# Moving the third batch's last twenty scatters from the tail into the attention slots of a two-layer transformer kernel, and the last batch's norm ahead of them

## What is computed

```
x = _layernorm(x + _L1_attn_ref(x, ...), axis=-1)

logits = flat.astype(jnp.float32) @ router_w.T + router_bias
scores = jax.nn.softmax(logits, axis=-1)
topk_scores, topk_idx = jax.lax.top_k(scores, TOPK)      # TOPK = 4 of E = 32
```

## Time and profile before

| | us |
|---|---|
| median of 3 runs | 1424.19 (1421.38 to 1424.64) |
| the profiled execution | 1412.93 |
| its span, from first to last instruction | 1410.9 |
| TensorE busy in the span | 1062.7 |
| VectorE busy | 785.1 |
| ScalarE busy | 516.9 |
| GpSimd busy | 507.8 |
| mean granted clock of TensorE | 0.872 |

### The profile page before, as it was taken

How to read it: one execution, slowest core, us unless ns; L and a number is a source line. 1 busy time by engine, 2 the same in 40 slices (tenths; PEclk the granted TensorE clock), 3 DMA queues, 4 the chain that set the end, 5 groups by cost and what they waited for, 6 DMA issues and landing times. The chain is left out here.

```text
span 1410.9 us, 20679 instructions
## 1 busy us (share of the span) xinstructions
PE 1062.7 (75%) x6895; PEld 625.1 (44%) x6896; DVE 785.1 (56%) x2075; ACT 516.9 (37%) x814; POOL 507.8 (36%) x542
## 2 busy tenths in 40 slices
PE   5762159815899999899999989884675976667676
PEld 4661137602344444444454434422443865556443
DVE  4757820145767877778777887841431433232326
ACT  1330014312265566565666556453211311111113
POOL 3110055066035103600154114342453366665633
PEclk9975569955599999999999999997698999998998
DMA  4226015213212121311232122015231422322135
GB/s 114 81 60 116 1 35 145 71 37 106 70 27 85 46 48 34 93 37 48 66 95 67 42 72 59 21 62 232 73 95 46 108 80 80 83 73 63 36 106 193
DMA packets 90022, 106.09 MB, mean 75 GB/s; under 512 B 16883, under 2 KB 69884, under 8 KB 87286
## 3 DMA queue, kind: packets, MB, share of 16 engines
q1 hardware_dynamic: 76502, 78.49, 19.3%
q0 software_dynamic: 13072, 25.90, 6.6%
q10 hardware_dynamic: 360, 0.59, 0.1%
HBM read 63.29 MB, written 37.95 MB: 72 GB/s over the span
## 5 line engine op out<-in xcount | busy, mean ns | idle before, releaser
L2005 DVE TENSOR_REDUCE maxima<-psum 128x1 f32<-128x512 f32 (+4 forms) x624 | 390.3, 644 | 116.7 <-PE psum L1826 62.7
L1944 ACT ACTIVATE probs<-psum 128x1024 f32<-128x1024 f32 (+3 forms) x384 | 300.2, 809 | 280.9 <-PE psum L1841 218.5
L1821 PE MATMUL psum<-ka,qa 75*128 75x512 bf16 (+3 forms) x768 | 242.5, 348 | 33.4 <-DVE maxima L2005 21.2
L1837 PE MATMUL psum<-qa,ka 78*128 78x512 bf16 (+3 forms) x768 | 206.7, 332 | 4.3 <-ACT probs L1944 2.1
L116 POOL DMA_INDIRECT expert_out<-g_y,g_place x160 | 155.2, 970 | 124.0 <-DMA expert_out<-g_y,g_place 56.2
L1854 PE MATMUL psum<-probs,v_wide 128*32 128x512 f32 (+3 forms) x1536 | 167.9, 510 | 0.0
L1821 PEld LDWEIGHTS psum<-ka,qa 75*128 75x128 bf16 x768 | 68.6, 99 | 178.2 <-DVE maxima L2005 137.3
L1358 POOL DMA_INDIRECT got<-expert_out,to_row x64 | 64.9, 1015 | 162.7 <-ACT probs L1944 103.5
L2480 DVE TENSOR_TENSOR g_y<-psum,g_gate 128x512 f32<-128x512 f32 x40 | 27.7, 691 | 156.2 <-DMA expert_out<-g_y,g_place 146.5
L1837 PEld LDWEIGHTS psum<-qa,ka 78*128 78x128 bf16 x768 | 74.4, 100 | 76.2 <-ACT probs L1944 28.2
L1841 PE MATMUL psum<-mask_k,ident_b 128*128 128x128 bf16 x512 | 104.4, 224 | 0.0
(11 more groups left out here) (325 smaller groups left out, 1646.1 us busy)
## 6 DMA issues: line engine op xcount, KB each, us to landing
g_rows<-sorted SPq DMA_DIRECT2D x160, 65.0 KB, 1.9
qa<-q_steps SPq DMA_DIRECT2D x45, 192.0 KB
ka<-k_steps SPq DMA_DIRECT2D x15, 576.0 KB
f_got<-expert_out SPq DMA_DIRECT2D x16, 512.0 KB, 11.1
w<-in_W SPq DMA_DIRECT2D x16, 256.0 KB
w_gu<-in_gu SPq DMA_DIRECT2D x1, 4096.0 KB, 18.1
q_steps<-q_parts SPq DMA_DIRECT2D x12, 256.0 KB
k_steps<-k_parts SPq DMA_DIRECT2D x12, 256.0 KB
```

The source lines that it names most:

```text
L1821: mm = pe.matmul(bank[:, h * width:(h + 1) * width], qa[b][0:ROWS_MAX, h0 + h, qt * P:(qt + 1) * P], ka[b][0:ROWS_MAX, h0 + h, seg * HALF: ...
L1837: mm = pe.matmul(out, ka[s.buf][0:ROWS_ALL, h, j * P:(j + 1) * P], qa[s.buf][0:ROWS_ALL, h, q0:(c + 1) * HALF], start=True, stop=True, ski ...
L1944: act.activation(probs[k % PRING][:, 2 * pair:2 * pair + 2, 0:w], PS[:, 2 * pair:2 * pair + 2, 0:w], ACT.Exp).then_inc(exps, 1)
L2005: dve.tensor_reduce(maxima[:, seg, h0:h0 + heads, qt], bank[:, 0:heads * width].rearrange("p (h k) -> p h k", h=heads), AX.X, ALU.max).the ...
```

## The change

The tuple `Finish` gets a field `beside`, the number of scatters in one slot. It is 1 for batches 0 and 1. Batch 2 gets 2, and its `paced` goes from 12 to all 32, so slots 32 to 47 of batch 3 hold two each. In the tail, `moves` then holds the 32 scatters of batch 3 alone, and `emit_norm` comes first in GpSimd's list.

```diff
-                 softmax=(20, 20), exp=21, choose=(22, 27), count=27, place=(29, 30), pick=(31, 42), scatter=32, paced=12)
+                 softmax=(20, 20), exp=21, choose=(22, 27), count=27, place=(29, 30), pick=(31, 42), scatter=32, paced=4 * TB, beside=2)
...
-                    k, t = divmod(r - f.scatter, TB)
-                    if 0 <= r - f.scatter < f.paced:
-                        if t == 0:
-                            emit_places1(pool, S, b, k)
-                        pool.wait_ge(exps, 2 * g)
-                        emit_scatter1(pool, S, b, k, t)
+                    for m in range(f.beside):
+                        k, t = divmod((r - f.scatter) * f.beside + m, TB)
+                        if 0 <= k * TB + t < f.paced:
+                            if t == 0:
+                                emit_places1(pool, S, b, k)
+                            pool.wait_ge(exps, 2 * g)
+                            emit_scatter1(pool, S, b, k, t)
...
-                for n, (b, k, t) in enumerate(moves):
-                    if n == TB:
-                        emit_norm(pool, S, 1, LAST)
+                emit_norm(pool, S, 1, LAST)
+                for b, k, t in moves:
```

More of the change, by code:

```diff
@@ L1109 @@
 BATCH_SLOTS = QUARTERS * SLOTS
-Finish = namedtuple("Finish", "turn_att proj moments scale each turn_new logits softmax exp choose count place pick scatter paced")
+Finish = namedtuple("Finish", "turn_att proj moments scale each turn_new logits softmax exp choose count place pick scatter paced beside")
 LATER = Finish(turn_att=(12, 13), proj=(15, 16), moments=(18, 24), scale=26, each=2, turn_new=(28, 30), logits=32,
-               softmax=(34, 35), exp=36, choose=(38, 45), count=45, place=(47, 49), pick=(50, 60), scatter=52, paced=4 * TB)
+               softmax=(34, 35), exp=36, choose=(38, 45), count=45, place=(47, 49), pick=(50, 60), scatter=52, paced=4 * TB, beside=1)
 AT_ONCE = Finish(turn_att=(4, 5), proj=(7, 8), moments=(10, 12), scale=14, each=4, turn_new=(15, 16), logits=18,
-                 softmax=(20, 20), exp=21, choose=(22, 27), count=27, place=(29, 30), pick=(31, 42), scatter=32, paced=12)
+                 softmax=(20, 20), exp=21, choose=(22, 27), count=27, place=(29, 30), pick=(31, 42), scatter=32, paced=4 * TB, beside=2)
 FINISH = {0: LATER, 1: LATER, 2: AT_ONCE}
```

## The result

The changed kernel is slower. In the first measurement the ratio of its time to the kernel before is 1.0106 (95% interval 1.0063 to 1.0150), medians 1442.26 against 1422.79 us. In microseconds the two ratios are +15.1 and +5.6, with +7.7 forecast in between. The medians are taken over all executions and the ratios over the fast ones alone; of the profiled executions that of `drain_in_between` was a slow one, and `all_landed` was executed only once. Single executions of either kernel scatter over 20 to 30 us, so the timed runs alone do not settle a term of a few microseconds. The profiles do, if they are read in pieces.

A forecast was written before the change was run, and what follows sets the result against it. Taken as bounding: GpSimd, whose DRAIN blocks end on and whose late norm stalls the tail 15.0 us. 22.0 (seam) + 0.7 (clock) - 15.0 (norm) = +7.7, 1424.19 to 1431.9 us; 8-in-10 range 1427 to 1439.

The forecast's parts named there:

- The copy: Before k = 1 in slot 36: GpSimd newly waits 5.0 us for batch 2's x_alt copy, held by batch 1's odd-k scatters.
- Slots 36 to 47: End of attention: 24 scatters with 21 gaps of 1.28 us and 2 of 2.10, the last starting at 981.27.
- the fifth rival: Slots 36 to 47: the scatter burst runs slower than 1.28 us each, up to +24.3, 1448.5 us; 8 in 100.
- The DRAIN: Attention's end: GpSimd's DRAIN ends 6.8 us after its last scatter starts (6.3 to 8.2), at 988.1.
- The seam: Between attention and tail: the tail opens 22.0 us later (21.5 to 23.4), waiting for GpSimd's DRAIN.
- The start of the tail: TensorE's two turnings before the variance both take 1.09 us after its long pause: +0.7 us (0 to 1).
- The third rival: Tail's turnings and router: TensorE's clock comes back sooner, saving 2.7 us, so +5.0, 1429.2 us; 7 in 100.
- The norm: In the tail: it waits only for the variance, at 1000.2, giving back 15.0 us; scatters behind it cost nothing.
- The rest: Shared block's loads, batch 3's 32 scatters and its copy: zero together, with 1 us either way.
- The first rival: At the seam other engines don't wait for GpSimd; norm starts at 982.3, time 1413.9 us; 4 in 100.
- The second: At the seam GpSimd's DRAIN takes only 0.31 us; sum +2.2, 1426.4 us; 5 in 100.
- The fourth: Before k = 1 the copy is not waited for: -5.0, so +2.7 and 1426.9 us; 3 in 100.

The follow-up runs named there:

- drain_in_between: Changed kernel with one more GpSimd DRAIN ahead of slot 26 of batch 3; ratio to the kernel before 1.0023 (0.9977 to 1.0069).
- all_landed: Changed kernel, GpSimd waiting for all scatters of batches 0 to 2 to land before attention ends; slot 32 to tail's end 168.9 us, single execution, no ratio.
- no_drain_at_seam: Changed kernel without GpSimd's DRAIN at attention's end, event exchange kept; ratio to the kernel before 0.9972 (0.9936 to 1.0008).
- norm_first_20_left: Kernel before with only the norm moved first in GpSimd's tail list, all 20 leftover scatters behind it; ratio to the kernel before 0.9973 (0.9930 to 1.0015).

## Why the prediction was right, and where not

Its direction and its mechanism hold: the moved scatters stretch attention by more than the earlier norm gives back. Step by step, in times from the first scatter of slot 32 or from the seam:

- *Slots 32 to 35.* Batch 1's last scatter 14.08 us after the first: it was 958.60 - 944.48 = 14.12.
- *The copy.* A wait of 5.0 us: 5.12, and removing its cause took 5.2 off the seam.
- *Slots 36 to 47.* The last scatter 52.25 us after the first: 52.39. The gaps stayed at 1.28, so the fifth rival fell.
- *The DRAIN.* **This term was mis-sized.** 6.8 us from the last start, with 6.3 to 8.2 kept as the range: it was 9.9, outside it. I had three rows, all with other counts of scatters, and took the middle one. They should have been read by what lay in each block: 20 more scatters in attention's make its own row of 8.2 longer by 20 x 0.082 = 1.6, which gives 9.8. The 0.082 was taken from the changed kernel, but a row of the kernel before gives it too, had I counted: 4.29 us behind the tail's 52 scatters.
- *The seam,* 22.0 us later: 25.2, all of the difference from the DRAIN.
- *The start of the tail,* +0.7 for the clock: the variance came 12.1 us after the seam in place of 11.4. The third rival, a sooner clock, fell: the router still took 3.60.
- *The norm.* It followed the variance by 0.09 us, and its chain to the places took 28.8 us against 29.1.
- *The rest,* forecast at zero: from the places to the last scatter 58.1 against 56.9 us, and the tail's own DRAIN 2.66 against 4.29, because 20 scatters had left that block. I had not seen that this DRAIN shrinks as the other grows.

Sum: 25.2 - 14.9 = +10.3, where +7.7 was forecast. The first rival (nobody waits for GpSimd) is refuted by the events at 1006.8, right behind GpSimd's DRAIN and 23 us behind VectorE's. The second (a short DRAIN) failed on the 8.9 us that the DRAIN took behind the last issue. The rule of the Trainium skill that the prediction set beside it (VectorE: DVE Perf Modes, The DRAIN you can't avoid) speaks of the DRAINs of the runtime's preamble and postamble. Those measured here stand at the ends of the kernel's own blocks, and `no_drain_at_seam` took one out with an option of the block. The prediction was therefore wrong to say that the trace disagrees with the rule: the rule speaks of other DRAINs, and it was no ground for the rival either. The fourth (no wait for the copy) only came about when the buffer was doubled.

One sentence was true of the kernel before and no more: that the scatters behind the norm cost nothing. They did while the norm was late. `norm_first_20_left` shows that they would have taken 11 of 14 us as soon as it was early. The move of scatters is therefore what makes the early norm pay, but with 4 leftovers fewer, and the norm behind four of the rest, that was had already, and moving the other 16 cost more at the seam than it brought.

That one measurement gave +15.1 us and the other +5.6 is not explained by anything in the change; the two intervals overlap, and single executions scatter by more. The first median, 1442.26 us, lies above the forecast range of 1427 to 1439. That the second, 1431.83, is almost exactly the 1431.9 of the forecast is luck: the profiles put the difference at +10.3 us, not +7.7. The 11.3 us between the profiled and the timed executions, for which the prediction had no reason, come from the short execution that was profiled; single timed ones go down to 1411.3.

## What to carry to other kernels

Work that seems free on an idle engine has a deadline at the next barrier; count the engine's own time to that point, its waits and its closing DRAIN included, against the slack (here 2.9 us), and move only as much as fits. When a step is pulled ahead of others on an in-order engine, ask when those others are needed next: fill exactly the time for which the step would wait. Where executions differ by more than the effect, cut the profiles at the last common instruction and compare stretches.

## What the runs showed of the hardware

- GpSimd's DRAIN at a block's end takes time even when everything has landed. Behind scatters of 128 rows of 520 bytes that time grew with their number: 2.66 us behind 32, 3.97 behind 48, 4.29 behind 52, and 8.87 behind 96 of them and 64 gathers. It repeats to a hundredth of a microsecond (2.66 in both profiles of the changed kernel). Another kind costs less: 3.96 us behind the experts' 160 scatters of 512-byte rows, 0.025 each.
- It also waits for what has not landed: it ended with the landing of a plain DMA of 2080 KB, after 22.3 to 24.1 us, and 1.7 us after the last of 40 gathers had landed.
- Why a DRAIN has such work, whether it goes by DMAs, rows or bytes, and why a block without a DRAIN left only 0.66 us more for the next, stays open; no run took that apart.
- GpSimd's sequencer ran five scatters ahead of its engine at the seam of the changed kernel: its DRAIN is shown from 991.6, and the last five scatters start from 991.77 to 996.87. With the DRAIN left out, the events at the block's end went out 6.2 us before GpSimd had finished its last scatter (992.62 + 0.97 against 987.4).
